# Finishing and routing chunks of nodes between stretches of the edge loop, with one-hot slot lists and gathered expert rows

## What is computed

```python
def _L0_gnn_ref(x, src, dst, Wq, bq, Wk, bk):      # x is layernormed
    q = jnp.tanh(x @ Wq + bq)
    k = x @ Wk + bk
    w = jnp.sum(q[s] * k[d], axis=1) / d_k
    ew = jnp.exp(w - wmax[d])
    alpha = ew / denom[d]
    out = jax.ops.segment_sum(alpha[:, None] * x[s], d, num_segments=N)
...
def _L0_ffn_ref(x, gamma, beta, Wr, br, W1, b1, W2, b2):   # x is layernormed again
    logits = jnp.einsum('bsd,de->bse', xn, Wr) + br
    top_vals, top_idx = jax.lax.top_k(logits, K)           # K = 2 of E = 8 experts
    w = jax.nn.softmax(top_vals, axis=-1)
    for e in range(E):
        h = jax.nn.gelu(jnp.einsum('bsd,dh->bsh', xn, W1[e]) + b1[e], approximate=False)
        y_e = jnp.einsum('bsh,hd->bsd', h, W2[e]) + b2[e]
        y = y + y_e * w_full[..., e, None]
...
x = x + _L0_gnn_ref(_layernorm(x, axis=-1), ...)
x = x + _L0_ffn_ref(_layernorm(x, axis=-1)[None], ...)[0]
```

## Time and profile before

| what | value |
|---|---|
| median of three runs | 1734.29 us |
| the profiled execution: its time, its span | 1731.01 us, 1729.4 us |
| busy in the span: PE, DVE, ACT, POOL | 64%, 43%, 30%, 63% |
| edge loop, by the slices of the page | from about 92 to 1170 us |
| finishing and routing | from about 1170 to 1332 us |
| experts | from about 1332 us to the end |

### The profile page before, as it was taken

One profiled execution on the slowest core, in us unless ns is written; L12 is line 12 of the kernel. 1 busy time (PEld: TensorE's weight loads), 2 busy tenths in 40 slices (PEclk: granted clock), 3 DMA queues, 4 the chain that ended last, 5 costly groups with the idle time before them and its releaser, 6 DMA issues. The chain is left out here.

```text
span 1729.4 us, 29512 instructions
## 1 busy us (share of the span) xinstructions
PE 1113.9 (64%) x6619; PEld 763.4 (44%) x6620; DVE 744.6 (43%) x2949; ACT 521.2 (30%) x1461; POOL 1088.6 (63%) x1100
## 2 busy tenths in 40 slices
PE   6735565566456556555555555554451999999997
PEld 5622232233223223222222222234451888888886
DVE  7724444444444444444444444447651222222222
ACT  3522222222222222222222222221110334443333
POOL 2067777777777777777777777753774344444444
PEclk9856656665666566666666666665555999999999
DMA  9575444544445544454444444437754355444544
GB/s 193 123 188 130 130 128 128 130 129 127 132 128 127 129 130 129 130 129 127 130 129 129 130 129 128 128 90 197 212 164 129 67 98 96 93 95 71 120 74 61
DMA packets 161413, 217.75 MB, mean 126 GB/s; under 512 B 60586, under 2 KB 128624, under 8 KB 161261
## 3 DMA queue, kind: packets, MB, share of 16 engines
q0 software_dynamic: 63568, 158.86, 37.0%
q1 hardware_dynamic: 95302, 58.29, 14.6%
q10 hardware_dynamic: 2520, 0.36, 0.2%
HBM read 174.20 MB, written 42.75 MB: 125 GB/s over the span
## 5 line engine op out<-in xcount | busy, mean ns | idle before, releaser
L526 POOL DMA_INDIRECT arena_a<-rows_dram,idx x848 | 803.4, 947 | 329.2 <-issue 255.3
L1338 PE MATMUL pb<-arena_a,arena_b 128*64 128x257 f32 x1696 | 375.3, 620 | 0.7 <-ACT arena_b L1162 0.7
L1314 PE MATMUL pb<-ident,qs 128*128 128x128 f32 x212 | 70.2, 432 | 414.3 <-ACT qs L1147 414.3
L589 POOL DMA_INDIRECT out_dram<-arena_b,tokB x104 | 162.7, 1564 | 225.9 <-DVE arena_b L1029 210.1
L836 DVE SCALAR_TENSOR_TENSOR acc<-acc,alpha,pb 32x257 f32 x424 | 203.3, 480 | 108.6 <-issue 96.8
L1338 PEld LDWEIGHTS pb<-arena_a,arena_b 128*64 128x64 f32 x1696 | 178.9, 220 | 156.6 <-issue 154.2
L818 DVE CUSTOM_DVE_ANT_0 arena_b<-pb,mask,nmo 128x512 f32<-128x512 f32 x106 | 79.6, 751 | 366.1 <-PE pb L1323 359.6
L1314 PEld LDWEIGHTS pb<-ident,qs 128*128 128x128 f32 x212 | 29.5, 196 | 445.3 <-ACT qs L1147 426.2
L1431 PE MATMUL pb<-arena_b 128*128 128x256 f32 x832 | 191.1, 383 | 1.2 <-ACT arena_b L1221 1.2
L1439 PE MATMUL pb<-arena_b 128*128 128x256 f32 x832 | 188.2, 379 | 0.0
L1431 PEld LDWEIGHTS pb<-arena_b 128*128 128x128 f32 x832 | 160.1, 193 | 23.9 <-ACT arena_b L1221 1.6
(11 more groups left out here) (183 smaller groups left out, 1076.3 us busy)
## 6 DMA issues: line engine op xcount, KB each, us to landing
arena_b<-xe_dram SPq DMA_DIRECT2D x53, 260.0 KB, 3.3
arena_a<-rows_dram,idx POOLq DMA_INDIRECT x848
arena_b<-dst_dram SPq DMA_DIRECT2D x212, 64.0 KB
arena_b<-in_L_ffn_W_dram POOLq DMA_DIRECT2D x16, 512.0 KB, 6.3
rows_dram<-acc SPq DMA_DIRECT2D x14, 493.5 KB, 6.0
acc<-in_x_dram SPq DMA_DIRECT2D x13, 448.0 KB, 14.7
arena_a<-in_x_dram SPq DMA_DIRECT2D x13, 448.0 KB
out_dram<-arena_a SPq DMA_DIRECT2D x13, 448.0 KB
```

Source lines behind the costliest of these rows:

```text
L526: g.indirect_dma_start(out=xg[:, (s * 2 + x_) * G + j, :], out_offset=None, in_=rows_dram[:, :], in_offset=bass.IndirectOffsetOnAxis(ap=id ...
L589: g.indirect_dma_start(out=out[:, :], in_=ybuf[:, k, :], in_offset=None, out_offset=bass.IndirectOffsetOnAxis(ap=tokB[:, k:k + 1], axis=0) ...
L1314: last = nc.tensor.transpose(pb[0][:, x_ * P:(x_ + 1) * P], qs[:, x_, :, :].rearrange("p j s -> p (j s)"), ident[:, :])
L1338: last = mm(sums_bank[b][HP * x_:HP * x_ + HP, 0:W1COLS], probT[:, b, j * P + HP * x_:j * P + HP * x_ + HP], xg[:, (s * 2 + x_) * G + j, 0 ...
```

## The change

Chunks 0 to 5 are finished and routed inside the edge loop. As soon as all items that touch a chunk are done, the loop stops after a quad (`segment` reads where, lists `segl` and `segh`), all engines but GpSimd run `finished(c)` (sum, statistics, normalisation, logits), then one quad, then `route(c)`, and the loop goes on. GpSimd's own loop isn't cut. Only chunk 6 is finished and routed after the loop. There is one buffer each for x (`xr`) and for the rows, not two.

The normalised rows are no longer scattered to the experts' lists. SP stores them in order of the nodes in `xn_dram`. Instead a list of node numbers is made: for each of 14 (tile, choice) pairs of a chunk VectorE builds one-hot matrices, of the partition (128 columns, once times the low and once times the high part of the node number) and of the column (8 x 51 = 408 columns), TensorE multiplies them and VectorE adds the product to `ltok`. At the end eight copies make a flat list, and GpSimd gathers the rows of each block with two indirect DMAs, in the place of SP's load. The gathers of block i+2 are issued in front of the scatters of block i. SP's loops over the chunks are written out.

```diff
+            def store_x2(c):
+                sp.wait_ge(a_x2, CH * (c + 1))
+                sp.dma_start(x_tiles(out, c * HCH, CH), xr[0:HP, :, :]).then_inc(a_o, 16)
+                if c < NCH - 1:
+                    sp.dma_start(x_tiles(out, c * HCH + HALF, CH), xr[HP:P, :, :]).then_inc(a_o, 16)
...
+            for c in range(NCH - 1):
+                lo, hi = segment(sp, c)
+                with sp.Fori(lo, hi) as k:
+                    quad(k)
+                store_x2(c)
+                sp.wait_ge(a_xn, CH * (c + 1))
+                sp.wait_ge(a_o, 32 * (c + 1))
+                load_x(c + 1)
+                with sp.Fori(hi, hi + 1) as k:
+                    quad(k)
+                store_normal(c)
...
-            def scatter(c, b, k, last=False):
-                g.wait_ge(a_slot, c + 1)
-                g.sem_inc(tk_g, 1)
-                for u in range(CH):
-                    n = LAST if last and u == CH - 1 else P
-                    for r in range(2):
-                        g.indirect_dma_start(
-                            out=xe_dram[:, :], in_=rows[0:n, b, u, :], in_offset=None,
...
+            def gather_block(listed, taken=None):
+                if taken is not None:
+                    g.wait_ge(b_xt, taken)
+                    g.wait_ge(b_meta, taken)
+                g.wait_ge(b_lx, listed)
+                g.sem_inc(tk_g, 1)
+                for k in range(2):
+                    g.indirect_dma_start(
+                        out=xrows[:, k, :], out_offset=None, in_=xn_dram[:, :],
+                        in_offset=bass.IndirectOffsetOnAxis(ap=gidx[:, k:k + 1], axis=0)).then_inc(b_rl, 16)
+
+            gather_block(1)
+            gather_block(2, 1)
...
                 with g.Fori(lo, hi) as i:
+                    gather_block(g.to_reg(i + 3), g.to_reg(i + 2))
                     for k in range(2):
                         g.wait_ge(b_yb, i * 2 + k + 1)
...
+                for u in range(CH):
+                    lo_col, hi_col = ((tt[:, c * CH + u:c * CH + u + 1] if last else tt[:, bass.ds(c * CH + u, 1)])
+                                      for tt in (toklo, tokhi))
+                    for r in range(2):
+                        i = 2 * u + r
+                        if i >= 4:
+                            v.wait_ge(a_lm, c * PAIRS + i - 3)
+                            v.sem_inc(tk_v, 1)
+                        v.tensor_scalar(ab[:, i % 4, 0, :], iota16[:, 0:P], spart[:, r, u:u + 1], lo_col, ALU.is_equal, ALU.mult)
+                        v.tensor_scalar(ab[:, i % 4, 1, :], iota16[:, 0:P], spart[:, r, u:u + 1], hi_col, ALU.is_equal, ALU.mult)
+                        v.tensor_scalar(bb[:, i % 4, :], iota16[:, :], scol[:, r, u:u + 1], None, ALU.is_equal).then_inc(a_ab, 1)
+                v.wait_ge(a_lm, (c + 1) * PAIRS)
+                v.sem_inc(tk_v, 1)
+                v.tensor_tensor(ltok[:, :], ltok[:, :], pb[6][:, 0:LCOLS], ALU.add).then_inc(a_ls, 1)
...
+            v.wait_ge(s_seg, 2)
+            with v.Fori(0, NCH - 1) as c:
+                lo, hi = segment(v, c)
+                with v.Fori(lo, hi) as k:
+                    quad(k)
+                v.wait_ge(s_acc, v.to_reg(hi * 4 + 3))
+                v.sem_inc(tk_v, 1)
+                finished(c)
+                with v.Fori(hi, hi + 1) as k:
+                    quad(k)
+                route(c)
...
+            for e in range(NE):
+                lo, _ = expert_ends(v, e)
+                if e:
+                    v.wait_ge(b_lf, e)
+                    v.sem_inc(tk_v, 1)
+                v.tensor_copy(lflatf[:, bass.ds(lo * 2, ECOLS)], ltok[:, e * ECOLS:(e + 1) * ECOLS]).then_inc(b_lf, 1)
...
+            pe.wait_ge(s_seg, 2)
+            with pe.Fori(0, NCH - 1) as c:
+                lo, hi = segment(pe, c)
+                with pe.Fori(lo, hi) as k:
+                    quad(k)
+                finished(c)
+                with pe.Fori(hi, hi + 1) as k:
+                    quad(k)
+                route(c)
```

More of the change, by code:

```diff
@@ L64 @@
 ITEMS_AFTER = 4
-ICOLS = 80
+ICOLS = 81
 ITEMS = P * ICOLS
@@ L388, in _, with quad @@
+            load_x(0)
+            sp.sem_inc(a_rw, 32)
+            sp.wait_ge(s_seg, 2)
+            def quad(k):
                 number = counter(sp, k)
@@ L847, in _, with quad @@
             add_sums(0, tiles, 0, XSLOTS + 1, 2)
-            n_quads = quad_count(v)
-            with v.Fori(0, n_quads) as k:
+            def quad(k):
                 number = counter(v, k)
@@ L980, in _ @@
-            route(NCH - 1, 0, last=True)
+                step(v.tensor_copy(slots[:, :, :], slotf[:, :, :]))
+                v.wait_ge(a_v, steps())
+                step(v.tensor_scalar(slots[:, :, :], slots[:, :, :], 7, None, ALU.arith_shift_right))
+                v.wait_ge(a_v, steps())
+                step(v.tensor_copy(scol[:, :, :], slots[:, :, :]))
+                v.wait_ge(a_v, steps())
+                v.scalar_tensor_tensor(out=spart[:, :, :], in0=scol[:, :, :], scalar=-float(P), in1=slotf[:, :, :],
+                                       op0=ALU.mult, op1=ALU.add).then_inc(a_slot, 1)
@@ new lines, in _ @@
+            lo, hi = segment(v, NCH - 1)
+            with v.Fori(lo, hi) as k:
+                quad(k)
+            n_quads = quad_count(v)
+            n_items = kept(v, n_quads * 4 + PEEL, NG // 2, ITEMS)
+            _, tiles, _ = item_reader(v, n_quads)
+            add_sums(1, tiles, 1, v.to_reg(n_items + XSLOTS), v.to_reg(n_items + 1))
+            v.wait_ge(s_acc, n_items + 2)
+            v.sem_inc(tk_v, 1)
+            v.memset(lflatf[:, :], 0.0).then_inc(b_lz, 1)
+            finished(NCH - 1, last=True)
@@ L983, in _ @@
+            route(NCH - 1, last=True)
             v.wait_ge(a_slot, NCH)
@@ L1174, in _, with quad @@
                 item(tiles, i, number, 32 * G)
-            n_quads = quad_count(a)
-            with a.Fori(0, n_quads) as k:
+            def quad(k):
                 number = counter(a, k)
@@ L1351, in _ @@
             pe.wait_ge(s_m0, 1)
-            number = counter(pe, 0)
-            item(0, number, first=True)
-            item(1, number)
-            n_quads = quad_count(pe)
-            with pe.Fori(0, n_quads) as k:
-                number = counter(pe, k)
-                for j in range(4):
-                    item(PEEL + j, number)
-            n_items = kept(pe, n_quads * 4 + PEEL, NG // 2, ITEMS)
-            sums(1, 1, pe.to_reg(n_items), pe.to_reg(n_items))
-            pe.wait_ge(s_acc, n_items + 2)
-            pe.sem_inc(tk_p, 1)
             pe.wait_ge(a_wr, 4)
```

422 lines of the change are left out of this document (250 added, 172 removed).

## The result

The changed kernel takes 1749.46 us in the median (1742.54 to 1750.88), the kernel before beside it 1733.64 (1731.02 to 1738.07): a ratio of 1.0081, 95% interval 1.0046 to 1.0115. So it is 0.8% slower, where the forecast had it 0.2% faster. The profiled execution of the changed kernel is the fastest of its runs, 1742.54 us with a span of 1740.9.

A forecast was written before the change was run, and what follows sets the result against it. GpSimd's gathers were taken to bound the edge loop, 10.0 us an item. 1731.0 - 113 + 84 + 3.6 + 1.5 + 20 = 1727, on the median's footing 1730; likeliest range 1710 to 1750, 8 in 10 for 1685 to 1795.

The forecast's parts named there:

- Stalls by SyncE's path: Edge loop: GpSimd waits for index loads queued behind SP's stores, and briefly for the sums; 14 us a chunk, +84.
- What would show it: The forecast's list of signs, such as two GpSimd gaps a chunk ended by the index load, about 10 and 3 us.
- PE's own work needs no more: Finishing a chunk in the loop: PE's 16.4 us end at T+48.4, before GpSimd's delayed gather at T+49.7; no extra loss.
- Slow issues beside the additions: Edge loop: a scatter beside additions to x takes 0.3 us longer; counted for gathers twice a chunk, +3.6 (0 to 6).
- Preparation: Ahead of the edge loop: some 10 small VectorE steps before the rows are stored, +1.5.
- The stage behind the loop: From the last sums to the experts' first transposition, only chunk 6 left: 50 us in place of 162.8, so -113.
- The experts: Expert loop: GpSimd gathers replace SP's load; +5 in steady blocks, +15 at seven changes of expert, together +20.
- lateness in steady blocks: Expert loop: gathered rows land slightly after PE wants them, 0.1 us a block, +5 (0 to +30).
- Rival 1: SP between store and index loads: store and load of x land late, 21 us lost a chunk, 1772; chance 0.18.
- Rivals 2 and 3: Faster: shorter loop stalls, experts' gathers mostly hidden, 1692, chance 0.27. Slower: gathers late in every expert block, 1756, chance 0.10.
- Rival 4: Edge loop: by the port rule VectorE's comparisons stop GpSimd writing descriptors, +60, 1790; chance 0.04.
- Rival 5: Chunks count as reached only near the edge loop's end, so 34 us each is not covered, 1822; chance 0.04.

## Why the forecast was nearly right and still on the wrong side

It was made of two large terms that all but cancel, and its mechanism was right for both. Several small terms were taken too low or not at all, and their sum is the difference between 1730 and 1749. The measured 1749.5 is at the very edge of the likeliest range, 1710 to 1750, and the forecast itself gave slower, 0.40, the same chance as faster.

1. **Stalls by SyncE's path, +84.** Measured 83.5, two gaps a chunk, each ended by the index load, as "What would show it" had it. Less the usual 0.3 the first is 9.5 in the mean, with 9.7 forecast; the second 4.4, where 3.3 by SyncE and 1 by the chain were taken. The index load ends it alone, so that their sum fits is partly luck. The store lands in 7.1 us (289.61 to 296.71), 6.7 taken. The remark that PE's own work needs no more is right only with SyncE late: without that the gaps that PE ends are 3.8 and 6.1 us in the first chunk. The forecast's own numbers held that already (sums 5.6 us after T+48.4, a gather wanted at T+50), but it was no term, as it was covered.
2. **Slow issues beside the additions, +3.6.** Mis-sized, and for another reason. The gathers took 8.8 us more (812.2 against 803.4). 50 of them were over 0.97 us, together 4.4 us over the usual, and 15 such, 1 us, were in the kernel before. So the term itself, 3.6, is about what came. The rest, some 6 ns on each of 848 or 5 us, had no term. It is there with no chunk in the loop too; its cause stays open.
3. **Preparation, +1.5.** 2.2 in the profiled execution, but the later ones of this preparation have their first gather at 97.3 to 98.4, with 92.3 and 94.4 for the kernel before: 3 to 6 us, for which no run isolated a cause. It may be what makes the median worse than the profile.
4. **The stage behind the loop, 50.** Measured 53.2. Finishing took 16.4 as taken (1267.45 to 1283.89), comparisons, products and the last addition 10.9 (1289.60 to 1300.54), 11 taken. What was mis-sized are the eight copies: 1.5 us each, 12 in all, where 9 stood with bounds of 5 to 13. The other steps together are 0.3 over.
5. **The experts, +20.** Measured 23.9. The 5 us of lateness in steady blocks did not come; blocks stayed at 7.345. The seven changes cost 21.8 and not 15: the gathers behind the wait for the scatter's landing start 5.4 us after that scatter (1426.25 to 1431.69), where 4.0 was taken. The 4.0 of the earlier trace rows was counted from the start of the scatter, and it runs from its end: 1427.83 to 1431.69 is 3.9. PE, which transposed the block ahead at 1425.65 and wanted this one at 1433.0, has it at 1435.8. To this come the three blocks at a lower clock, 5.2 us, for which the forecast had nothing.
6. **Small gaps.** Five waits under 1 us in the catching up behind a chunk, 2.3 us without the usual 0.3 each, were not in the sum. With them the loop's 95.0 us are 83.5 + 8.8 + 2.3 and 0.4 that the rows don't place.

By the profiled executions: 97.2 - 109.6 + 23.9 = +11.5, where -3.9 stood: 8.1 in the loop and ahead of it, 3.4 behind it, 3.9 among the experts. By the medians it is +16. The failed step is the sizing of the small terms of the sum, above all three: a change of expert at 2.1 us, which measured 3.1 (+6.8); the gathers' issues at +3.6, which measured +8.8; and the copies of the list at 9, which measured 12. Within their bounds they weren't taken low (9 is the middle of 5 to 13), but a landing was counted from the wrong end, and the even growth of every gather and the clock behind a wait had no term. With a margin of 4 us between terms of 113 and 84 they decide the sign.

**The rivals.** Rival 1 (store and load land late) didn't come: 13.9 us lost a chunk, under its 14.7. Rivals 2 and 3 didn't either. Rival 4 says that comparisons stop GpSimd: the excess of long gathers is 4.4 us over the whole loop, not 60. Of the 30 gathers beside comparisons 18 take 0.95 to 0.97 us, 11 up to 1.07, and one, which also stands beside the list's addition, 1.20. So a comparison lengthens a gather by some 0.1 us or, mostly, not at all. Beside the normalisation (L964) 12 of 14 gathers take 0.99 to 1.08, and the longest two, 1.23 and 1.28, stand beside the additions to x. The warning of the Trainium skill ("SBUF — State Buffer", on DVE blocking DMA) would have had GpSimd locked out for their length; for comparisons of int16 with a bf16 result this trace doesn't show it, and no row says in which mode they ran. Rival 5 didn't come: chunks were reached through the loop, with their first gaps ending at 305.8, 482.1, 658.1, 793.2, 969.1 and 1145.5.

As for the Trainium skill's sentence that a ring is consumed in order ("DMA: Bandwidth & Descriptors", Queues, rings and completion order): at 1427.3 the weights are issued, at 1431.7 and 1433.0 the gathers, and PE has their rows at 1435.8, 1.8 us after the last issue ended (1434.03). That is no later than in the edge loop, where it was 2.5 us; whether the weights had landed by then the rows don't show.

## What to carry to other kernels

When work is moved into a loop that one engine bounds, ask for each piece how long it holds the other engines at a stretch, and compare that with what the buffers between them bridge; the loop hides many short stalls and only part of a long one, of the same sum. Look through the in-order queues first: here 30 us of the loss was a wait for a store that stood ahead of loads of the next items, and another 22 a wait for scatters ahead of gathers, with the lower clock behind it. When two large terms cancel, the sign hangs on the small ones: give each a term, count a landing from the end of its issue, and call the sign open while the margin is smaller than their bounds.

## What the runs showed that was not expected

The same kernel takes 1733 us in some sets of runs and 2047 and 2059 in others. In the traces of the changed kernel nearly all of the difference is in the edge loop, 1589.2 us against 1173.9, where an item takes 12.6 us and not 10.0; the experts take 425.0 against 421.6. The products' recorded durations reach the same values in both (L1466: 635 ns in the median), but what waits for them starts later, and the profile names no releaser. SyncE's queue is slower as well: its register operations for the target loads (L360) take up to 1.43 us there, against 0.11, and one pair of such loads 5.83 us (at 714.87), against 1.35 to 2.45. Whether GpSimd or the chain sets the pace of a loop can therefore change from one set of runs to another, and with it the worth of interleaving: it saved 110 us against everything behind the loop in one, and cost 27 in the other. Why the pace differs stays open: no experiment was made on it, and the chip's number doesn't separate the two.

Two register loads and a copy on VectorE take 1.5 us for each expert, of which the copy is 0.19; the edit that leaves one of the loads out gave 0.6 us a copy.
